# Attention on one core: ScalarE copies 192 score pieces to bf16 for pairwise maxima on VectorE, and the weighted values of two steps stand in one block with three probability buffers

## The reference

```python
qkv = jnp.einsum('bsi,oi->bso', x, w_qkv) + b_qkv
q, k, v = jnp.split(qkv, 3, axis=-1)            # per head, 16 wide
attn = jnp.einsum('bhqd,bhkd->bhqk', q, k) * scale
attn = jax.nn.softmax(attn, axis=-1)
vals = jnp.einsum('bhqk,bhkd->bhqd', attn, v)
```

## Time and profile before

| | us |
|---|---|
| median of 3 runs (lowest, highest) | 1539.56 (1530.76, 1542.15) |
| span of the profiled execution, first to last instruction | 1412.3 |
| median less span: start, end and what the profile leaves out | 127.3 |
| the 256 steps of attention, first exponential to the last step's | 726.1 |

### The profile page before, as it was taken

One profiled execution on the slowest core, in us unless ns is written; L12 is line 12 of the kernel. 1 busy time (PEld: TensorE's weight loads), 2 busy tenths in 40 slices (PEclk: granted clock), 3 DMA queues, 4 the chain that ended last, 5 costly groups with the idle time before them and its releaser, 6 DMA issues.

```text
span 1412.3 us, 30839 instructions
## 1 busy us (share of the span) xinstructions
PE 1342.8 (95%) x8191; PEld 672.8 (48%) x8192; DVE 1134.9 (80%) x2823; ACT 753.7 (53%) x1155; POOL 606.9 (43%) x782
## 2 busy tenths in 40 slices
PE   7997999999999999999999999999999999999895
PEld 4552222332333323323333232568788888888551
DVE  7886999999999999999999994566566656656588
ACT  3762477676767676777677768113343433334100
POOL 4000113143644534636346357527755555655300
PEclk9997799999999999999999999999999999999999
DMA  6898355533546345444464355947766665666698
GB/s 218 260 270 216 93 171 133 121 85 83 125 126 156 91 121 149 132 96 107 125 170 117 105 155 176 274 136 234 231 199 206 202 183 177 180 179 178 238 344 337
DMA packets 216958, 243.55 MB, mean 172 GB/s; under 512 B 93948, under 2 KB 181500, under 8 KB 216736
## 3 DMA queue, kind: packets, MB, share of 16 engines
q1 hardware_dynamic: 189328, 166.42, 43.6%
q0 software_dynamic: 21776, 68.07, 13.4%
q10 hardware_dynamic: 5760, 7.87, 1.7%
HBM read 133.98 MB, written 108.28 MB: 172 GB/s over the span
## 4 chain that ended last, share of the span: by engine, by line
PE 71%; DVE 13%; DMA 4%; issue 1%; SPq 1%; ACT 1%; POOL 0%; DVEq 0%; POOLq 0%
PE psO L1174 14%; PE ex_psGU L1682 13%; PE psE L1161 13%; PE psM L1151 9%; DVE piece_max L1048 9%; PE ex_psY L1697 7%; PE ex_psX L1671 3%; PE psM L505 2%; PE ex_psA L1691 2%; PE psGU L1495 1%; DMA wide<-results 1%; PE co_psS L1951 1%; PE late_psGU L1931 1%; PE late_psX L1942 1%; PE psM L524 1%
## 5 line engine op out<-in xcount | busy, mean ns | idle before, releaser
L1048 DVE TENSOR_REDUCE piece_max<-psM 128x1 f32<-128x512 f32 x1024 | 641.9, 680 | 27.3 <-PE psM L1151 24.0
L1115 ACT ACTIVATE wide<-psE 128x1024 f32<-128x1024 f32 x512 | 496.8, 1021 | 206.2 <-PE psE L1161 204.1
L1151 PE MATMUL psM<-wide 48*128 48x512 bf16 x1024 | 324.0, 395 | 19.9 <-DVE piece_max L1048 11.7
L1161 PE MATMUL psE<-wide 49*128 49x512 bf16 (+1 forms) x2048 | 328.7, 380 | 3.2 <-DMA wide<-maxima 2.8
L1763 POOL DMA_INDIRECT results<-vals_inv,places x223 | 213.9, 959 | 150.5 <-DVE vals_inv L1749 86.4
L1174 PE MATMUL psO<-wide 128*32 128x512 f32 x2048 | 273.6, 606 | 0.6 <-ACT wide L1115 0.6
L1151 PEld LDWEIGHTS psM<-wide 48*128 48x128 bf16 x1024 | 78.1, 93 | 348.1 <-DVE piece_max L1048 277.3
L1682 PE MATMUL ex_psGU<-wide,ex_xT 128*128 x892 | 231.3, 382 | 0.8 <-ACT ex_xT L1714 0.7
L1161 PEld LDWEIGHTS psE<-wide 49*128 49x128 bf16 (+1 forms) x2048 | 117.6, 95 | 92.3 <-issue 8.7
L1682 PEld LDWEIGHTS ex_psGU<-wide,ex_xT 128*128 128x128 f32 x892 | 152.1, 190 | 14.6 <-issue 2.3
L1714 ACT ACTIVATE ex_xT<-ex_psX 128x256 f32<-128x256 f32 x223 | 85.3, 383 | 121.3 <-PE ex_psX L1671 118.5
(11 more groups left out here) (281 smaller groups left out, 1262.8 us busy)
## 6 DMA issues: line engine op xcount, KB each, us to landing
wide<-qk_parts SPq DMA_DIRECT2D x384, 64.0 KB
wide<-results SPq DMA_DIRECT2D x16, 1536.0 KB, 9.5
rows<-lists SPq DMA_DIRECT2D x112, 160.0 KB
h2Ts<-lists SPq DMA_DIRECT2D x111, 160.0 KB
qk_parts<-parts SPq DMA_DIRECT2D x32, 384.0 KB, 3.1
xin<-in_x_dram SPq DMA_DIRECT2D x16, 512.0 KB, 4.2
v_values<-vst SPq DMA_DIRECT2D x32, 256.0 KB, 3.5
wide<-v_values SPq DMA_DIRECT2D x16, 512.0 KB
```

The lines of the kernel that those rows point to most:

```text
L1048: v.tensor_reduce(piece_max[:, qh, (x * PAIRS + h) * KT // QH + qt, kh:kh + 1], bank_of("piece", PIECES * group + n), AX.X, ALU.max, negat ...
L1115: nc.scalar.activation(probs[:, step % 2, 2 * pair:2 * pair + 2], psE[:, pair], ACT.Exp, scale=HD ** -0.5).then_inc(exp_ok, 1)
L1151: nc.tensor.matmul(bank_of(*user), qa[g][rows, h, qt * P:(qt + 1) * P], ka[g][rows, h, kh * 512:(kh + 1) * 512], start=True, stop=True).th ...
L1161: mm = nc.tensor.matmul(psE[:, pair, x], k[g][part, pair, kt * P:(kt + 1) * P], q[g][part, pair, qh * 512:(qh + 1) * 512], start=(q is qa) ...
```

## The change

1. ScalarE copies. Of each half's 32 pieces, six (piece 2 of the steps that fill places p = 0, 1, 2, 4, 5, 6 of a half; the pieces of step *s* fill place p = (s + 3) mod 8) are no longer reduced by DVE. ACT copies each, 128 x 512, from `psM` to bf16 in SBUF (`hold`), behind the two exponentials of the step, and the piece three later waits for this copy. That is 192 pieces of 1024.
2. Pairwise maxima. DVE joins three held pieces at a time (`join`): three `tensor_tensor` maxima in place, of 3 x 256, 3 x 128 and 3 x 64 elements, and one `tensor_reduce` of 3 x 64. Triple 0 is joined at place p = 4, triple 1 at p = 7.
3. The weighted values of two steps form a block: at even steps those of the two steps before, at odd steps none.
4. Three probability buffers instead of two; the third is `h2Ts`. The exponential of a step waits for the weighted values three steps back. For this the loads of `h2Ts` for the closing phase wait for `summed` of the last step but one, and some scratch moves to parts of `x2` and `act_s`.

```diff
+    HELD_PIECE, HELD_STEPS, TRIPLE = 2, (0, 1, 2, 4, 5, 6), 3
+    JOINED_IN = {4: 0, 7: 1}
...
-            sp.wait_ge(spare_in, 16 * (E + 1))
+            sp.wait_ge(summed, ALL - 1)
...
+            def join(half, triple, level):
+                of = held[triple]
+                if level < 3:
+                    width = 256 >> level
+                    if level == 0:
+                        dve.wait_ge(piece_held, TRIPLE * (2 * half + triple + 1))
+                    else:
+                        chain.ready()
+                    chain.then(v.tensor_tensor(of[:, :, 0:width], of[:, :, 0:width], of[:, :, width:2 * width], ALU.max))
+                else:
+                    chain.ready()
+                    at = HELD_STEPS[TRIPLE * triple]
+                    v.tensor_reduce(piece_max[:, half % QH, at:at + TRIPLE, HELD_PIECE // 2], of[:, :, 0:64], AX.X, ALU.max,
+                                    negate=True).then_inc(joined, 1)
+
+            def piece_or_join(group, n):
+                if not held_at(n):
+                    piece_maximum(group, n)
+                p, r = n // 4 % STEPS_HALF, n % 4
+                if p in JOINED_IN:
+                    half, triple = QH * group + n // HALF_PIECES, JOINED_IN[p]
+                    for level in ((0,), (1, 2), (3,), ())[r]:
+                        join(half, triple, level)
...
+            def hold(group, n):
+                at = held_before(PIECES * group + n)
+                triple, slot = divmod(at, TRIPLE)
+                act.wait_ge(piece_done, PIECES * group + n + 1)
+                if slot == 0:
+                    wait(act, joined, triple - 1)
+                nc.scalar.activation(held[triple % 2][:, slot], bank_of("piece", PIECES * group + n), ACT.Copy
+                                     ).then_inc(piece_held, 1)
...
-                        wait(act, summed, step - 1)
-                    nc.scalar.activation(probs[:, step % 2, 2 * pair:2 * pair + 2], psE[:, pair], ACT.Exp,
+                        wait(act, summed, step - 2)
+                    nc.scalar.activation(probs[step % 3][:, 2 * pair:2 * pair + 2], psE[:, pair], ACT.Exp,
...
+                for n in range(first, first + 4):
+                    if to < NGR and held_at(n):
+                        hold(to, n)
...
-                if c == "piece":
-                    pe.wait_ge(piece_read, w + 1)
+                if c == "piece" and held_at(w % PIECES):
+                    pe.wait_ge(piece_held, held_before(w + 1))
+                elif c == "piece":
+                    pe.wait_ge(piece_read, read_before(w + 1))
...
-                if step:
+                if step and step % 2 == 0:
+                    weighted_values(step - 2)
                     weighted_values(step - 1)
...
+            weighted_values(ALL - 2)
             weighted_values(ALL - 1)
```

More of the change, by code:

```diff
@@ L736, in attention_phase @@
     PAIRS = HG // 2
+    STEPS_HALF = HALF_PIECES // 4
+    HELD_PIECE, HELD_STEPS, TRIPLE = 2, (0, 1, 2, 4, 5, 6), 3
+    JOINED_IN = {4: 0, 7: 1}
     NGR = B * NG
@@ L743, in attention_phase @@
         qa, qb, ka, kb, va = env.qa, env.qb, env.ka, env.kb, env.va
-        probs = env.wide[:, GPART * NG:].rearrange("p (n h q) -> p n h q", n=2, h=HG)
+        probs = [*(env.wide[:, GPART * NG + HG * 512 * n:GPART * NG + HG * 512 * (n + 1)].rearrange("p (h q) -> p h q", h=HG)
+                   for n in range(2)), env.h2Ts[:].rearrange("p n k t -> p (n k) t")]
         o_sb = sb("o_sb", [P, HD, S // HD], F32)
@@ L747, in attention_phase @@
         inverse = sb("inverse", [HG * HD, S // HD], F32)
-        spare_to = env.h2Ts[:, 0].rearrange("p k t -> p (k t)").bitcast(I32).rearrange("p (e f) -> p e f", e=E)
+        spare_to = env.x2[:, TPC * (LAST - 1):TPC * LAST].rearrange("p i d -> p (i d)").bitcast(I32).rearrange(
+            "p (e f) -> p e f", e=E)
         piece_max = sb("piece_max", [P, QH, COLS, 2], F32)
+        held = [of.bitcast(BF16)[:, 0:TRIPLE * 512].rearrange("p (n k) -> p n k", n=TRIPLE)
+                for of in (env.act_s[:].rearrange("p m t -> p (m t)"),
+                           env.x2[:, TPC * LAST:].rearrange("p i d -> p (i d)"))]
         neg_max = sb("neg_max", [P, HG * KT], BF16)
@@ L754, in attention_phase @@
         psO = ctx.enter_context(nc.psum_tensor("psO", [P, 512], F32))
-        (scored, exp_ok, summed, piece_done, piece_read, max_ready, max_stored, max_there, o_read,
+        (scored, exp_ok, summed, piece_done, piece_read, piece_held, joined, max_ready, max_stored, max_there, o_read,
          o_stored, den_stored, den_in, divided, inv_stored, ch) = (
-            env.sem("att_" + n) for n in ("scored", "exp_ok", "summed", "piece_done", "piece_read",
+            env.sem("att_" + n) for n in ("scored", "exp_ok", "summed", "piece_done", "piece_read", "piece_held", "joined",
                                           "max_ready", "max_stored", "max_there", "o_read", "o_stored", "den_stored", "den_in", "divided", "inv_stored", "chain"))
@@ L780, in chunk_at, with held_at, held_before, read_before @@
             return c - 1, w
+        def held_at(n):
+            return n % 4 == HELD_PIECE and n // 4 % STEPS_HALF in HELD_STEPS
+        def held_before(n):
+            halves, n = divmod(n, HALF_PIECES)
+            return len(HELD_STEPS) * halves + sum(held_at(m) for m in range(n))
+        def read_before(n):
+            return n - held_before(n)
         ring = Ring(HALF_PIECES, PIECES * NGR)
@@ L786, in bank_of @@
             return psM[:, ring.bank[user]] if user in ring.bank else None
+        env.pieces_read = read_before(PIECES * NGR)
         def pieces_for(step):
@@ L1017, in _ @@
             add_bias(0)
+            pool.wait_ge(spare_in, 16 * (E + 1))
             for c in range(LAST):
@@ L1053, in finish @@
                 cols = slice(COLS * (k % QH), COLS * (k % QH + 1))
-                dve.wait_ge(piece_read, HALF_PIECES * (k + 1))
+                dve.wait_ge(piece_read, read_before(HALF_PIECES * (k + 1)))
+                dve.wait_ge(joined, 2 * (k + 1))
                 chain.link(v.tensor_tensor(neg_max[:, cols], part[:, :, 0], part[:, :, 1], ALU.min))
@@ L1075, in _ @@
             for n in range(HALF_PIECES):
-                piece_maximum(0, n)
+                piece_or_join(0, n)
             dve.wait_ge(env.zeroed, 1)
@@ L1087, in _ @@
                     if group < NGR:
-                        piece_maximum(group, first + n)
+                        piece_or_join(group, first + n)
                 if group < NGR and (first + 4) % HALF_PIECES == 0:
@@ L1108, in beside @@
                     half_scores(act, env, c, bank_of(c, w))
+            def hold(group, n):
[6 more added lines that the diff above has]
+                                     ).then_inc(piece_held, 1)
+            for n in range(HALF_PIECES + 4 * AHEAD):
+                if held_at(n):
+                    hold(0, n)
             for step in range(ALL):
@@ L1122, in _ @@
                     copy_out(group - 1, 1)
+                to, first = pieces_for(step)
+                for n in range(first, first + 4):
+                    if to < NGR and held_at(n):
+                        hold(to, n)
             copy_out(NGR - 1, 1)
@@ L1174, in weighted_values @@
                     mm = nc.tensor.matmul(psO[32 * h:32 * h + 32], va[g][:, kt, 32 * h:32 * h + 32],
-                                          probs[:, s % 2, 2 * pair + x], start=(kt == 0), stop=(kt == KT - 1))
+                                          probs[step % 3][:, 2 * pair + x], start=(kt == 0), stop=(kt == KT - 1))
                 mm.then_inc(summed, 1)
```

2 lines of the change are left out of this document (1 added, 1 removed).

## The result

The changed kernel takes 1717.7 us (median of 4 runs, 1704.7 to 1726.3) against 1540.7: ratio 1.116, interval 1.108 to 1.124. It is slower, as forecast, but by 177 us and not by 101, and outside the range. On another chip it was timed again against 1417.2 and takes 1612.2 there, ratio 1.138 (1.135 to 1.141), +195.

What follows compares the result with a forecast made beforehand. PE and DVE were both taken to be within 0.1 us of the step, with ACT having slack; 14 + 73 + 9 + 3.7 + 1 = 101 us more on 1539.6 gave 1640 us, range 1556 to 1676.

Steps and rivals of the forecast that it cites:

- The two-step chain and the banks: Clean steps of attention: exponentials and late-freed PSUM banks make PE wait, so a half takes 24.2 us against 20.2.
- The first 32 steps: Start of attention, all clean steps, 84.78 us before: +14, after some 2 us for waits for maxima that longer steps hide.
- the 5.49 of the chain: Two clean steps with only the exponential making PE wait: 5.49 us against 4.98; as a rival 1579, chance 0.20.
- The price of a join: DVE's pair maxima and short reduction for three held pieces: 2.2 us at f32 rows' price, against 1.8 for three reductions.
- the lower bound: Join priced at 1.4 us, halving the part by columns; level 0 is 0.49 and pair s = 1, 2 takes 6.10.
- A period: 32 attention steps with routing, 93.33 us before: +9.7 for 20 clean steps, +2.5 for mixed; six periods +73.
- Contention: GpSimd (POOL) slowing DVE's joins with two SBUF inputs: another 10 us within the rival on mixed steps, priced by no row.
- All mixed steps suffer: Rival for steps beside routing: +7 a period in place of +2.5, 27 us more, 1667; chance 0.15.
- The ends: Pieces ahead of the first step, and the later loads of h2Ts before the closing phase: together +1 us.
- DVE below 85% in attention: Sign the forecast is right: DVE's busy share in attention falls below 85%, all its idle time in the block.
- The wait list: Sign the forecast is right: PE's scores wait for ACT and its pieces for the copies.
- The base: Span of 1412.3 us plus 127.3 around it, to which the forecast added 101 us.

Runs made afterwards that it cites:

- copies alone: The changed kernel with weighted values back in every step, so copies and joins without the block: ratio 1.0765 against the kernel before, +106 us.

## Why the prediction was off

The direction and its cause in clean steps were right; the size was not. By its own steps:

- *The two-step chain and the banks, 24.2 a half*: held. Pairs (3,4) and (7,0) took 5.52 and 5.53 where 5.69 was worked out, (5,6) 6.37 for 6.28, (1,2) 6.10 for 6.51; the half 23.5. The scores of pair 1 wait for the exponential at 2.67 for 2.65, and the block takes 1.85 for 1.90. The first 32 steps cost +11.6 in one trace and +14.1 in the other, for +14. With the block alone the banks are the tighter limit: 5.73 a pair, where the exponentials alone would give 5.49. So banks and exponential stand close together, and the 5.49 of the chain was never seen by itself.
- *The price of a join*: too high, and the bound was the truth. Level 0 lasts 0.55, not 0.96, so the pair (1,2) is the 6.10 of the lower bound. Levels of 768 and 384 columns differ by 0.20, which is 0.5 ns a column where the f32 rows had 1.05. The Trainium skill ("VectorE: DVE Perf Modes", the perf-mode tier table) had twice the rate for bf16 `tensor_tensor` between SBUF tiles, and the trace agrees. By that rule alone the forecast would have been 1630, farther from the result, since the error lay elsewhere.
- *A period, +9.7 for 20 clean steps and +2.5 for the mixed ones with bounds 0 and 7*: this step failed. A period cost 26.4, 14.2 above the forecast of 12.2: the 20 steps +14.1, as w = 18 to 20 had been counted among the clean ones, and the mixed ones +12.4, beyond their upper bound. 12 of the 14.2 lie in w = 18 to 24: +17.0 where 5.1 had been worked out (9.7 / 20 for each of three steps, and 1.6 and 2.0). I had followed only the waits, each at its price at full speed. At w = 21 to 24 the waits were not too small, 2.3 of PE's idle time for 3.6; the other 6.6 is PE busy longer over the same 106 records, at 0.70. Six periods account for 88 of the 90 us by which attention missed the 101. Two things were missing.
- *Contention*, named in the rival with 10 us and left unpriced. Each level's length less its length alone, summed over the 192, is 43 us in this trace, 38 of them at w = 17 to 20. Cutting GpSimd's operations took 20 us off these lengths and gave back 38 us of time, so a stretched level cost more than its own length. The Trainium skill ("SBUF — State Buffer", "Who interferes with whom") says that a DVE instruction with two SBUF inputs contends with GpSimd's reads; the trace agrees, with 2.3 to 2.4 us for a level of 0.26 or 0.35 beside a GpSimd operation of 2.36. The right sum would have asked which joins meet GpSimd's 128 x 1024 operations.
- *The clock* was in no step and in no rival. The 102 us by which PE's busy time in attention grew are more than half of the 191. The windows of before show 0.96 in the first 32 steps and 1.00 over attention, and I took it for given that a change that makes PE wait costs the wait alone. The experiments show where it falls: at w = 21 to 24, never without block and copies there, always with the block, and with copies in all periods or (one reduction a join) in half of them; with GpSimd shortened, at w = 18 to 20 in one period of six. With copies alone the fall at w = 10 comes right behind a wait of 2.52. A small clock loss is no sign of a small cost: with the one reduction and no block the time rose by 89 us though PE's busy time in attention rose by 9.5 only.
- *All mixed steps suffer* (1667) was the nearest rival, for another reason than DVE's order.
- *The ends*, +1: nothing is seen; the buffers alone are 1.001. *DVE below 85% in attention*: it is 75% (690.78 of 917.42). *The wait list*: PE's matmuls wait for ACT and for copies as forecast, but the 69.5 us for reductions are far more than the 6.8 for the copies in `act_s` and the 3.9 of the scores.
- *The base*: "127.3 around the span" was the difference of two chips. It did not change the difference forecast, only what it meant.

What stays open: how much of the 102 us is clock alone, since PE's records overlap less or more as its order changes; and why the clock falls at w = 21 to 24 while clean steps, where PE is idle too (2.6 us of 23.9 at w = 0 to 7), keep 1.00 from the third period on at the latest. With the block alone it falls to 0.93 in such steps in three of the six periods. Copies without joins were not run, so their share by themselves is not shown.

## What to carry to other kernels

Where PE is 95% busy and its clock full, price a change by the waits it adds to PE *and* by what follows if the clock falls: look for the stretches that are already uneven (here the routing's steps) and ask whether the change adds a wait just there. A moved operation is to be placed against the other engines' timeline, not only into its own: the same joins and their copies cost 106 us where they stood and 60 us spread, and 12 us in 12 of 32 halves at clean steps, where 40 would be their share. And first count what an engine can win at all: some 25 us of DVE time was all that the joins could save.

## What the runs showed that was not expected

- A DVE maximum of 384 or 192 bf16 columns per partition, both operands in SBUF, lasts 0.35 or 0.26 us alone and up to 2.9 us beside a GpSimd `tensor_tensor` of 128 x 1024 f32 (2.36 us); it ends 0.1 to 0.2 us after that one. With copies alone one of 384 lasted 3.15 though it began 0.56 ahead of the `tensor_tensor`, during a GpSimd indirect DMA that ended just before it.
- A DVE reduction of 512 bf16 values from SBUF lasts 0.68 us, as one of 512 f32 values from PSUM (0.68 us): bf16 did not speed up a reduction.
- PE at a mean granted clock of 0.57 over 7.8 us without any wait, and at the lower clock weighted values of one step 1.93 in place of 1.06 us.
- The same kernel spends 533 us behind attention on one chip and 632 on another.
